# A mixture-of-experts kernel on one core: the down products two slices behind, weights late, and a loop unrolled

## The reference

```python
x = x + tanh(g_xattn) * attn(layernorm(x), ctx)        # x: 4 x 256 x 256
x = x + tanh(g_ffn) * moe(layernorm(x))                # 1024 tokens, 256 wide
# attn: kv = ctx @ W_k.T + b_k; out = p @ kv; sim = out @ kv.T / 16
#       sim normalised over its row, * gamma + beta, softmax
# moe:  scores = sigmoid(h @ gate_weight.T) for 16 experts; the two best of four groups,
#       the best four experts of these; their weights normalised, times 2.5
#       sum over experts of w * (silu(h @ g.T) * (h @ u.T)) @ d.T, and a shared expert of width 256
```

## Time and profile before

| | |
|---|---|
| median of the runs | 194.6 us |
| the profiled execution | 194.61 us, its span 192.8 us |
| TensorE busy | 183.1 us, 95%, 1003 matmuls |
| VectorE busy | 147.1 us, 76% |
| ScalarE, GpSimd busy | 81.2 us (42%), 83.0 us (43%) |
| granted TensorE clock | full in all 40 slices |

### The profile page before, as it was taken

One profiled execution on the slowest core, in us unless ns is written; L12 is line 12 of the kernel. 1 busy time (PEld: TensorE's weight loads), 2 busy tenths in 40 slices (PEclk: granted clock), 3 DMA queues, 4 the chain that ended last, 5 costly groups with the idle time before them and its releaser, 6 DMA issues.

```text
span 192.8 us, 3265 instructions
## 1 busy us (share of the span) xinstructions
PE 183.1 (95%) x1003; PEld 151.9 (79%) x1003; DVE 147.1 (76%) x332; ACT 81.2 (42%) x160; POOL 83.0 (43%) x101
## 2 busy tenths in 40 slices
PE   6999799969899999999999989999999999999993
PEld 5665457858788888888788868888888888888882
DVE  1759988989899699998469999885666665566664
ACT  2449725523248833435457333434334343433220
POOL 2352162822841755553345543454444555444410
PEclk9999999999999999999999999999999999999999
DMA  5967200002785555541221000312211221221403
GB/s 145 344 212 217 76 0 0 0 0 57 235 205 183 150 141 163 161 139 58 54 54 54 0 3 9 109 57 74 80 60 54 54 54 60 74 78 60 143 20 112
DMA packets 10297, 18.08 MB, mean 94 GB/s; under 512 B 1773, under 2 KB 3821, under 8 KB 10286
## 3 DMA queue, kind: packets, MB, share of 16 engines
q1 hardware_dynamic: 9504, 17.11, 29.4%
q10 hardware_dynamic: 782, 0.83, 1.8%
HBM read 16.82 MB, written 1.11 MB: 93 GB/s over the span
## 4 chain that ended last, share of the span: by engine, by line
PE 67%; DVE 20%; DMA 6%; issue 2%; POOL 1%; ACT 1%; DVEq 0%; SPq 0%; POOLq 0%
PE bank L782 41%; PE bank L834 8%; PE bank L826 7%; PE bank L828 7%; DMA xs<-x_in 3%; DVE act_hi L553 2%; DVE bank L556 2%; DVE act_lo L561 2%; DMA w_row<-weight_rows 2%; DVE stats L458 1%; POOL rstd L278 1%; PE bank L712 1%; DMA weight_rows<-w_blk 1%; DVE beats L597 1%; PE bank L752 1%
## 5 line engine op out<-in xcount | busy, mean ns | idle before, releaser
L284 POOL TENSOR_TENSOR w_lo<-w_raw,w_hi 128x256 fp32r<-128x256 f32 (+1 forms) x72 | 72.4, 1024 | 76.7 <-ACT w_hi L327 75.6
L327 ACT CAST w_hi<-w_raw 128x256 fp32r<-128x256 f32 (+2 forms) x72 | 36.5, 513 | 56.4 <-PE bank L834 30.6
L782 PE MATMUL bank<-hT_hi,w_hi 128*128 128x512 f32 x142 | 56.5, 398 | 0.0
L782 PE MATMUL bank<-hT_lo,w_hi 128*128 128x512 f32 x142 | 56.0, 395 | 0.0
L782 PE MATMUL bank<-hT_hi,w_lo 128*128 128x512 f32 x142 | 44.7, 396 | 0.0
L535 DVE TENSOR_TENSOR weighted<-bank,w_row 128x512 f32<-128x512 f32 x30 | 20.7, 691 | 25.6 <-ACT bank L386 24.5
L826 PE MATMUL bank<-w_hi,act_hi 128*128 128x256 f32 x144 | 36.0, 283 | 1.8 <-DVE act_hi L553 1.8
L828 PE MATMUL bank<-w_lo,act_hi 128*128 128x256 f32 x144 | 35.8, 281 | 0.0
L782 PEld LDWEIGHTS bank<-hT_hi,w_lo 128*128 128x128 f32 x142 | 26.7, 188 | 6.3
L782 PEld LDWEIGHTS bank<-hT_hi,w_hi 128*128 128x128 f32 x142 | 26.8, 189 | 5.1
L826 PEld LDWEIGHTS bank<-w_hi,act_hi 128*128 128x128 f32 x144 | 27.2, 189 | 4.3 <-issue 2.8
(11 more groups left out here) (100 smaller groups left out, 133.2 us busy)
## 6 DMA issues: line engine op xcount, KB each, us to landing
w_row<-weight_rows SPq DMA_DIRECT2D x31, 256.0 KB, 3.2
w_raw<-w_in SPq DMA_DIRECT2D x18, 384.0 KB, 3.9
xs<-x_in SPq DMA_DIRECT2D x4, 256.0 KB, 5.9
out<-x SPq DMA_DIRECT2D x2, 256.0 KB, 3.5
cw<-ctxw_in ACTq DMA_DIRECT2D x1, 276.2 KB
vec<-vecs_in ACTq DMA_DIRECT2D x1, 265.0 KB, 5.6
out<-x SPq DMA_DIRECT2D x2, 128.0 KB, 1.8
out<-x ACTq DMA_DIRECT2D x2, 128.0 KB, 1.8
```

The costliest lines, as they stand in the source:

```text
L284: nc.gpsimd.tensor_tensor(w_lo[:, par, cols], w_raw[:, bass.ds(n, 1), cols].rearrange("p o c -> p (o c)"), w_hi[:, par, cols].bitcast(F32) ...
L327: nc.scalar.copy(w_hi[:, par, cols], w_raw[:, bass.ds(n, 1), cols].rearrange("p o c -> p (o c)"))\
L782: last = nc.tensor.matmul(dst, w[:, par, w0 + c * P:w0 + (c + 1) * P], m, start=i == 0, stop=i == len(parts) - 1, skip_group_check=True)
```

## The change

- `act_hi`, `act_lo` and the down weights (`d_hi`, `d_lo`, new tensors) get three buffers instead of two; the gate and up weights keep two.
- TensorE's step k does gate(k), up(k), down(k-2); after the last step come down(34) and down(35).
- ScalarE and GpSimd prepare the down weights of slice k in step k (`high_d(k)`, `low_d(k)`), two steps before down(k).
- Slices 2 and 3: VectorE's step only multiplies up by silu from PSUM into `weighted` in SBUF and signals `act_done`; row and split follow later in `late_parts`, both after step 3. Up(4) and up(5) wait for `act_done` instead of `act_lo`.
- VectorE's table: ranking, masking and picking all after step 1; `sim_stats(2)` and `sim_centre(2)` from before the loop to after step 2; batch 3's centring from step 2 to 4. `first_row` moves from gate(3) to gate(4). Results 0 and 1 come one step later.
- GpSimd's `root(1, 2)` moves from before the loop to after step 2, `root(1, 3)` from step 2 to 3.
- The loops are written out on all engines. SP asks for a weight row after `act_lo` instead of `act_done` of the slice that last used its buffer, loads rows 1 and 2 first, and then the ninth slice of weights.

```diff
-            straight(0, NF + 2)
-            loop(NF + 2, 2 * NF - 2)
-            straight(2 * NF - 2, 2 * NF)
+            for k in range(2 * NF):
+                step(k, k % 2)
+                for piece in between.get(k, ()):
+                    piece()
...
+            for r in (1, 2):
+                load_row(r, r % 2)
+            for r in range(3, E):
+                n = r + ahead - 3
+                if n < NF:
+                    sp.wait_ge(w_in[n % 2], 16 * (n // 2))
+                    load_slice(n, n % 2)
...
+                sp.wait_ge(actlo_done, r - 1 + NSH)
+                load_row(r, r % 2)
...
+            def weighted_late(k, par):
+                ins = nc.vector.tensor_tensor(weighted[:, par, :], up_ps[par][:, :], weighted[:, par, :], ALU.mult)
+                ins.then_inc(act_done, 1)
+                dve.wait_ge(act_done, k + 1)
+            def late_parts(k):
+                par, own = k % 2, k % 3
+                if k == NSH:
+                    dve.wait_ge(first_row_done, 1)
+                    row = first_row_ps[:, :]
+                else:
+                    dve.wait_ge(row_in[par], 16)
+                    row = w_row[:, par, :]
...
+                nc.vector.tensor_tensor(act_hi[:, own, :], row, weighted[:, par, :], ALU.mult).then_inc(acthi_done, 1)
+                link(nc.vector.tensor_tensor(weighted[:, par, :], row, weighted[:, par, :], ALU.mult))
+                dve.wait_ge(acthi_done, k + 1)
+                nc.vector.tensor_tensor(act_lo[:, own, :], weighted[:, par, :], act_hi[:, own, :].bitcast(F32),
+                                        ALU.subtract).then_inc(actlo_done, 1)
...
-                0: [rank_groups, mask_groups],
-                1: [lambda: pick_experts(0)],
-                2: [lambda: sim_stats(3), lambda: sim_centre(3)],
-                4: [lambda: sim_logits(2, 9)],
+                1: [rank_groups, mask_groups, lambda: pick_experts(0)],
+                2: [lambda: sim_stats(2), lambda: sim_centre(2)],
+                3: [lambda: late_parts(2), lambda: sim_stats(3), lambda: late_parts(3)],
+                4: [lambda: sim_centre(3), lambda: sim_logits(2, 9)],
...
-                    pe.wait_ge(actlo_done, k - 1)
+                    pe.wait_ge(act_done if k - 2 in WEIGHTED_LAST else actlo_done, k - 1)
...
-                if first >= 1:
-                    down(k - 1, 1 - par, int(first - 1 >= NF), first - 1 in (0, NF))
+                if k >= 2:
+                    if k % NF == 2:
+                        pe.wait_ge(score_ready, k // NF + 1)
+                    down(k - 2)
```

More of the change, by code:

```diff
@@ L230, in _ @@
             sp.wait_ge(rows_out[0], 16)
[L231 to L242, removed]
+            for r in (1, 2):
[5 more added lines that the diff above has]
+                    load_slice(n, n % 2)
+                if r == E // 2:
+                    sp.wait_ge(rows_out[1], 16)
+                sp.wait_ge(actlo_done, r - 1 + NSH)
+                load_row(r, r % 2)
             write_rows(1)
@@ L245, in _ @@
                 sp.wait_ge(rows_out[c], 32)
[L246 to L249, removed]
+            for r in range(E, 2 * E):
+                sp.wait_ge(actlo_done, r - 1 + (NSH if r < E + 2 else 2 * NSH))
+                load_row(r, r % 2)
             for b in range(2):
@@ L279, in root, with low_gu, low_d, step @@
                   .then_inc(rstd_ready, 1)
[L281 to L300, removed]
+            def low_gu(k):
+                pool.wait_ge(hi_gu, k + 1)
+                nc.gpsimd.tensor_tensor(w_lo[:, k % 2, :], w_raw[:, k % NF, 0:GU], w_hi[:, k % 2, :].bitcast(F32),
+                                        ALU.subtract).then_inc(lo_gu, 1)
+            def low_d(k):
+                pool.wait_ge(hi_d, k + 1)
+                nc.gpsimd.tensor_tensor(d_lo[:, k % 3, :], w_raw[:, k % NF, GU:WCOL], d_hi[:, k % 3, :].bitcast(F32),
+                                        ALU.subtract).then_inc(lo_d, 1)
+            def step(k, par):
+                if k + 2 < 2 * NF:
+                    low_gu(k + 2)
+                low_d(k)
             for b in range(B):
@@ L306, in _ @@
               .then_inc(gwlo_ready, 1)
-            low_gu(0, 0, 0)
+            low_gu(0)
             root(1, 0)
@@ L314, in _ @@
             pool.wait_ge(hid_ready[1], 2)
[L315 to L318, removed]
+            low_gu(1)
+            each_step(pool, step, {2: [lambda: root(1, 2)], 3: [lambda: root(1, 3)], 8: [lambda: root(2, 2)], 10: [lambda: root(2, 3)]})
         @block.scalar
@@ L379, in logit_exp, with step @@
                   .then_inc(score_ready, 1)
-            def step(k, par, first):
+            def step(k, par):
                 act.wait_ge(gate_done, k + 1)
-                routed = not shared_or_late(first)
-                if not routed and first >= 2:
+                routed = not shared_or_late(k)
+                if not routed and k >= 2:
                     act.wait_ge(act_done, k - 1)
[L386 to L395, removed]
+                nc.scalar.activation(gate_ps[par][:, :] if routed else weighted[:, par, :], gate_ps[par][:, :], ACT.Silu)\
+                  .then_inc(silu_done, 1)
+                if k in table_change:
+                    table_change[k]()
+                if k + 2 < 2 * NF:
+                    high_gu(k + 2)
+                high_d(k)
             table_change = {6: lambda: (softmax_exp(2), softmax_exp(3)), 15: lambda: logit_exp(1)}
@@ L808, in gate_up, with down @@
                 else:
-                    midway = first_row if first == NSH + 1 else None
+                    midway = first_row if k == NSH + 2 else None
                     product(k, gate_ps[par][:, :], 0, moving, par, midway).then_inc(gate_done, 1)
-                if first >= 2:
-                    pe.wait_ge(actlo_done, k - 1)
+                if k >= 2:
+                    pe.wait_ge(act_done if k - 2 in WEIGHTED_LAST else actlo_done, k - 1)
                 product(k, up_ps[par][:, :], C * P, moving, par).then_inc(up_done, 1)
-            def down(k, par, half, start, token_spans=spans(0)):
+            def down(k):
+                par, half, start = k % 3, k // NF, k % NF == 0
                 pe.wait_ge(hi_d, k + 1)
                 pe.wait_ge(lo_d, k + 1)
-                rows = slice(GU, WCOL)
-                for s, toks in enumerate(token_spans):
+                for s, toks in enumerate(spans(k)):
                     span = range(toks.start // P, toks.stop // P)
@@ L825, in down @@
                         own = slice(t * P, (t + 1) * P)
[L826 removed]
+                        nc.tensor.matmul(acc, act_hi[:, par, own], d_hi[:, par, :], start=start and t % 2 == 0,
                                          stop=False, skip_group_check=True)
[L828 removed]
+                        nc.tensor.matmul(acc, act_hi[:, par, own], d_lo[:, par, :], start=False, stop=False,
                                          skip_group_check=True)
```

112 lines of the change are left out of this document (44 added, 68 removed).

## The result

The changed kernel takes 197.22 us in the median of four runs (196.58, 196.59, 197.85, 198.31), the kernel before 194.59: a ratio of 1.0144, 95% interval 1.0087 to 1.0202. It is slower, as forecast (195.3), but by 2.6 us instead of 0.7, and outside the range of 193.8 to 196.5. The four runs fall in two groups, two at 196.6 with a mean granted clock of 0.998 and 0.999, two at 197.9 and 198.3 with 0.990 and 0.991. The profiled run is the slowest, 198.31, so its account against the profiled 194.61 of before is 3.7 us.

The account below looks back on a forecast made before the run. TensorE was taken as saturated except for gaps of at most 4.9 us, all caused by VectorE through act_hi or act_lo. +2.3 - 1.35 - 0.16 = +0.8, rounded down to +0.7 on 194.6, gave 195.3 us; eight in ten 193.8 to 196.5.

Parts of the forecast that it names:

- The mechanism: Start to gate(8): TensorE stands 0.6 at gate(4), 1.2 at the first row, 0.25 at gate(6), 1.15 at gate(7).
- The stop before the hidden transposes: Second half's hidden rows: TensorE arrives at 85.8, transposes start at 87.55, so it stands 1.7 us.
- silu(7): ScalarE after batch 3's logits: 3.79 us from third exponential to silu's end, ending at 66.25, 0.85 later than before.
- The waits for GpSimd at the start: VectorE before gate(8): 0.4 and 1.0 in ranking to picking, 0.6 by slice 3, 0.5 by batch 2's logits.
- Slices 15 to 18: Gate(15) to gate(20): no gap at gate(19), 1.35 of 1.6 us won, taking 21.4 us instead of 22.84.
- The tail's 0.16: Last down products: the 0.16 us gap is won, since the last act_lo is ready while down(34) runs.
- Gate(8) to the hidden rows: VectorE's 19.7 us after silu(7), plus 0.6 and 0.8 on two residuals; transposes at 87.55, 2.3 us behind.
- The rule that the prediction weighed: GpSimd blocking VectorE: the one-input normalisation could wait up to one subtraction; time about 195.9 instead of 195.3.
- VectorE wins its race: From picking to the transposes: picking ends at 42.2, gate(4) is not held; transposes at 85.3 give 193.2; chance 0.17.
- The prices cancel: Before the hidden rows: half the GpSimd waits don't come, transposes at 86.6, time 194.5; chance 0.36.
- A longer chain through the table load: At gate(8): batch 3's exponentials and the cast delay low_gu(8), holding TensorE; 1.2 more gives 196.5; chance 0.08.
- Unrolling: Former two-step loop: forecast nothing to win; the rival claimed 0.2 per pass over 7 passes, 193.9; chance 0.02.

Follow-up runs that it names:

- e2_clear: Changed kernel with GpSimd held once, before its gate and up subtraction for slice 14, until the last normalisation is done; 194.82 to 195.43 us, ratio 1.0007.
- e6_clear3: Changed kernel with GpSimd held at three places, until batch 2's residual, batch 3's residual and the normalisation are out; 192.68 to 193.05 us, ratio 0.989.
- e1_warm: Changed kernel with seven products of zeros on TensorE before the second half's hidden transposes; 196.39 to 196.79 us, ratio 1.0083.
- e3_front: Changed kernel with batch 2's statistics and centring, and GpSimd's root, back before the loop; 196.64 to 198.72 us, ratio 1.0135.
- e4_unroll: Kernel before with all its loops written out and nothing else changed; 194.69 to 196.49 us, ratio 1.0024.
- f6_fill_clear3: Changed kernel with three GpSimd holds, batch 2's centring before the loop, and logits earlier, batch 2's between slices 2 and 3; 191.8 to 192.42 us, ratio 0.9849.

## Why the prediction was right in direction and wrong in size

- *The mechanism* was right up to gate(8). The stops are where the forecast put them: gate(4) 0.31 (forecast 0.6), first row 1.06 (1.2), gate(6) 0.50 (0.25), gate(7) 0.55 (1.15). These are the rows' idle times; counted from when the product could have started, as the forecast counts, they are 0.1 to 0.2 longer (0.46, 1.21, 0.66, 0.71). Gate(7) starts at 60.17, forecast 60.2. The stop before the hidden transposes, 1.50 (forecast 1.7), came near by luck: the normalised rows let it go at 88.61, 1.06 later than the 87.55 of the forecast, and TensorE was there about as much later than its 85.8, since two small stops were added, 0.31 at 73.48 and 0.48 at 82.64, each behind a residual that met GpSimd. None is left in a down product.
- *silu(7)* ends at 66.17, forecast 66.25. ScalarE's timeline of the changed kernel has the chain as worked out: the exponential that waits for the logits, then silu.

```profile
62.36 0.51 ACT L339 ACTIVATE prob<-logit,neg_max 128x256 f32<-128x256 f32 x1 [2.55 <-DVE neg_max L471]
...
65.59 0.58 ACT L362 ACTIVATE bank<-bank 128x512 f32<-128x512 f32 x1
```

- *The waits for GpSimd at the start* were of the right size, at other instructions: masking 1.16 (0.94 of wait, forecast 1.0), slice 3's `act_lo` 1.72 (1.03 of wait, forecast 0.6), the logits of batch 2 none (forecast 0.5).
- *Slices 15 to 18* were right. Gate(15) at 101.55 to the last down products before gate(20), which start at 122.27, and the gate behind them gives 21.2 us, forecast 21.4, before 22.84. The tail's 0.16 is won.
- *The step that failed is "Gate(8) to the hidden rows".* In the sum I put 0.6 and 0.8 us on the two residuals and nothing on the normalisation and the scalings. The measured waits are 3.95: the residual pairs 0.43 each, the scalings 0.70 and 0.94, the normalisation 1.45. I had searched the rows for small work with two operands, and the scalings and the normalisation have one tensor as input. The normalisation's cover was gone once VectorE ran later: before, it ran from 83.75 to 85.12, and GpSimd's subtractions ended at 83.97 and began again at 86.19. A second, smaller error went the other way: I let TensorE wait for the last normalised row, but the transposes start behind the first two of the four, at 88.61, while the last are still being made. So of 2.55 us too little in the price, 1.75 reached gate(13) (4.05 against 2.3).
- *The rule that the prediction weighed* would have named the normalisation and the scalings. The Trainium skill, "SBUF — State Buffer", Who interferes with whom, says that a one-input VectorE instruction in a two-port mode is blocked for the whole of a GpSimd instruction that holds the shared ports. The prediction put 0.6 on it, outside the sum and for the normalisation alone. The traces agree with the rule: 2.82 us against 1.37 in e2_clear, where GpSimd is held, and the scaling of 128x2 elements 0.93 and 1.17 against 0.23 in e6_clear3. In which mode these instructions run no trace shows.
- *Not forecast at all* is the clock. The stop before the transposes was in the forecast, with 1.7 us, but nothing for what it does to the clock behind it: +1.62 us in the profiled run (4.42 against 2.80). e1_warm shows that it hangs on that stop, and e3_front that the stop does not always bring it.
- *The account.* 4.05 + 1.62 - 1.64 - 0.16 = 3.87, against 3.70 measured between the profiled runs. Without the clock it is 2.25, next to the 2.0 of the two runs at 196.6. With only the normalisation cleared, e2_clear takes 195.0 us, near the forecast of 195.3.
- *The rivals.* "VectorE wins its race" had its break-even at transposes of 86.75 and put 85.3 at 193.2; e6_clear3 starts them at 85.34 and takes 192.8. That sum holds, but what decided it was not picking, whose masking took 1.16 in the changed kernel, but GpSimd later on. "The prices cancel" wanted the transposes at 86.6; they start at 88.61. "A longer chain through the table load" did not come: no stop of TensorE stands at gate(8), which starts at 64.48. Unrolling gives nothing in e4_unroll. The Trainium skill, "Runtime: NRT & Kernel Launch", Instruction fetch mechanics, would have let it give something; 1.0024 (0.9995 to 1.0052) and the 63.30 us against 63.31 speak against that for these loops.
- *One reading of the code* was off: `high_d(k)` still waits for a down, down(k-3). ScalarE never stood for it (the page has no idle time before these casts), so nothing hung on it.

Still open is whether the four stops of 0.3 to 1.1 us between gate(4) and gate(7) could all go: f6_fill_clear3 trades them for one of 1.29.

## What to carry to other kernels

When a retiming moves VectorE work, lay GpSimd's timeline beside each moved instruction, the small ones and those with one input too, and price each overlap at what is left of the GpSimd instruction. Where GpSimd has slack, a wait that holds it until the urgent VectorE work is done is a cheap cure: three such waits turned a ratio of 1.0144 (1.0087 to 1.0202) into a gain of 1.1% (0.9864 to 0.9916). A stop of TensorE can cost twice, once for itself and once for the clock behind it: so it was, though not in every run, behind stops of 1.50, 2.00 with 1.13, and 2.25 us here.

## What the runs showed of the hardware

- A VectorE instruction of 128x2 elements took 1.17 us instead of 0.23 beside one GpSimd subtraction of 1.29 us.
- The granted clock behind a stop in an otherwise full stream: 0.76 over 7 us after 1.50 us (in two of four runs, by the mean clock; in the profiled run of e3_front 1.00 after 1.51), 0.57 over 4 us after 2.00 and 1.13, 0.63 over 4 us after 2.25. In f6_fill_clear3, whose longest stop among the steps is 1.29, all five runs have 0.997 to 1.0. Where between these the fall begins was not tried.
- The kernel before has a stop of 1.39 us, in front of down(1). In its profiled run the clock was 1.00 behind it; its timeline of TensorE:

```profile
41.02 0.35 PE L826 MATMUL bank<-w_hi,act_hi 128*128 128x256 f32 x1 [1.39 <-DVE act_hi L553]
```

But of the 40 runs of it that the experiments' ratios use, 12 have mean clocks of 0.987 to 0.991 and take 194.91 to 196.36 us, against 194.38 to 195.61 in the other 28. No profile of these 12 was kept, so which stop it was is open. They make part of the 1.1%: against the other runs of its round alone, e6_clear3 gains 1.0%.
